# A graph-attention kernel on one core: all seven slots of a tile summed by TensorE

## The chip, the core and the metric

The kernel runs on one core of a Trainium2 chip. The metric is the device time of one execution in microseconds (us). A core has five engines with a queue of instructions each, which run side by side and meet by semaphores: TensorE (PE, with its weight loads as PEld), VectorE (DVE), ScalarE (ACT), GpSimd (POOL) and SyncE (SP). SyncE here only issues DMAs; ScalarE and POOL issue some too. Matmul results go to PSUM, everything else lies in SBUF.

## What is computed

A graph-attention layer over 8192 nodes with 256 features, a residual and a layer norm:

```python
h = features @ W
s1 = h @ a1; s2 = h @ a2
e = leaky_relu(s1[:, None] + s2[None, :], negative_slope=0.2)
e = where(adjacency > 0, e, -9e15)
attention = softmax(e, axis=1)
out = layernorm(x + elu(attention @ h))
```

The adjacency matrix is 8192 x 8192 int32, 268 MB, and sparse: the chance of an edge falls with the row and column number, so that most rows have few edges and the first ones many.

## The kernel before

Rows are taken in 64 tiles of 128 (T = 64), two tiles make a pair (G = 32 pairs). The adjacency matrix is streamed once through SBUF, in 128 halves of a tile (2 MB each), and the few edges of a row are found without ever holding the row as floats. Work runs as follows.

**First phase** (to about 150 us): TensorE projects x to h, VectorE copies it out, POOL stores it row by row into a table `haug` in DRAM, with s1 and s2 as two more columns.

**The scan**, one step s per tile. ScalarE's `count` (L1317) turns a half of the adjacency tile into bf16. TensorE's `pack` (L529) multiplies it by powers of two into `pk` in PSUM, 16 matmuls per tile. VectorE's `scan` (L771 to L805) reads the column numbers of up to eight edges per row from it and writes `ids`. POOL's `gather` (L1499) fetches the rows of h for the first K = 7 of them, one indirect DMA per slot, into `GATH`, a ring of four tiles.

**The softmax over the slots** comes some steps later (`soft_step`; in four steps two tiles come at once). VectorE's `soft_logits` (L814 to L821) makes the logits, ScalarE's L1326 the exponentials, and VectorE's `soft_weights` the seven weights. The weighted sum of the seven gathered rows is split. For four slots (ON_PE) VectorE writes four diagonal matrices `diag` (L835) and TensorE's `slots` (L540) multiplies each with its gathered rows, adding up in a bank of `acc`. For the other three VectorE itself multiplies and adds into `PART` (L842, L845 twice). `aggregate` (L851) adds the two parts for a pair. ScalarE takes the exponential of the sum (L1337), VectorE's `residual` (L859 to L874) makes the elu and adds x, POOL makes the inverse standard deviation (L1511, L1513), VectorE's `normalise` (L880) finishes and SyncE stores the pair (L453).

**Rows with more than seven edges** are done densely in 16 chunks beside the scan (`mid_` functions): the first tile, and 128 listed rows. TensorE's part of it is a spread of s2 (L582), transposes (L596) and sums (L606), VectorE's among others L924 and L952, ScalarE's L1352, L1357 and L1368. In one of three steps TensorE has the sums and the spread behind the slots.

**The order** is written out by hand, per engine and step. TensorE: two packs, the slots of the step before, the dense pieces. VectorE: `normalise`, `soft_weights`, the scan, `soft_logits`, `residual`, `aggregate`, dense pieces. SyncE has one queue: the loads of the halves, each waiting until the count of three halves before is through (four buffers), and every store placed after a fixed load. After the last step VectorE's order for the last three tiles is written out singly.

```python
dve.wait_ge(sum_ready, t - 1)                     # diag(t): the sums of two tiles before
pe.wait_ge(agg_ready, j - 1)                      # slots of pair j: the addition of pair j - 2
pool.wait_ge(sum_ready, t - RING + 1)             # gather(t): the ring
pool.wait_ge(part_steps, PARTS * (t - RING + 1))
```

Of the kernel before, what the change touches and what calls it, by code (L numbers as in the profile page):

```python
# [23 lines left out]
ON_PE = 4  # L24
# [11 lines left out]
def gat_resnorm(nc, x, adj, W, attn, out):  # L36
# [21 lines left out]
    with ExitStack() as ctx:  # L58
# [26 lines left out]
        diag = sb("diag", [P, 2, 4, P], F32)  # L85
        PART = sb("PART", [P, 2, GROUP, D], F32)
# [73 lines left out]
        probsT = [diag[:, b, :, :].rearrange("p a b -> p (a b)") for b in range(2)]  # L160
# [102 lines left out]
        part_steps = sem("part_steps")  # L263
        sum_ready = sem("sum_ready")
        agg_ready = sem("agg_ready")
# [143 lines left out]
        PARTS = K - ON_PE  # L409
# [70 lines left out]
        def _(pe):  # L480
# [53 lines left out]
            def slots(t):  # L534
                j = t // 2
                pe.wait_ge(diag_ready, t + 1)
                if j >= 2:
                    pe.wait_ge(agg_ready, j - 1)
                for k in range(ON_PE):
                    done = nc.tensor.matmul(acc[:, j % 2, (t % 2) * D:(t % 2 + 1) * D], diag[:, t % 2, k, :],  # L540
                                            GATH[:, t % RING, k * DA:k * DA + D],
                                            start=(k == 0), stop=(k == ON_PE - 1))
# [193 lines left out]
        def _(dve):  # L736
# [87 lines left out]
            def soft_weights(t):  # L824


                r, b, j = t % RING, t % 2, t // 2
# [5 lines left out]
                if t >= 2:  # L833
                    dve.wait_ge(sum_ready, t - 1)
                dve.tensor_tensor(diag[:, b, 0:ON_PE, :], ident[:].unsqueeze(1).broadcast_to([P, ON_PE, P]),  # L835
                                  weight[:, 0:ON_PE].unsqueeze(2).broadcast_to([P, ON_PE, P]), ALU.mult)\
                    .then_inc(diag_ready, 1)
                part = PART[:, j % 2, b, :]
                for k in range(ON_PE, K):
                    rows = GATH[:, r, k * DA:k * DA + D]  # L840
                    if k == ON_PE:
                        dve.tensor_scalar(part, rows, weight[:, k:k + 1], None, ALU.mult).then_inc(part_steps, 1)  # L842
                    else:
                        dve.wait_ge(part_steps, PARTS * t + k - ON_PE)
                        dve.scalar_tensor_tensor(out=part, in0=rows, scalar=weight[:, k:k + 1], in1=part,  # L845
                                                 op0=ALU.mult, op1=ALU.add).then_inc(part_steps, 1)

            def aggregate(j):
                dve.wait_ge(sum_ready, 2 * j + 2)
                dve.wait_ge(part_steps, PARTS * (2 * j + 2))  # L850
                dve.tensor_tensor(PART[:, j % 2, :, :], acc[:, j % 2, :].rearrange("p (u d) -> p u d", u=GROUP),  # L851
# [835 lines left out]
```

## Time and profile before

| | us |
|---|---|
| median of 3 runs | 853.82 |
| lowest, highest | 851.44, 854.61 |
| the profiled execution | 854.12 |
| its span, first to last instruction | 852.3 |
| busy: PE, DVE, ACT, POOL | 602.2, 612.7, 578.0, 603.0 |

The four compute engines are each busy 68 to 72% of the span. The DMA engines moved 320 MB, 376 GB/s on average. A stretch's "DMA share" is the mean busy share of the 16 DMA engines, where 1.0 means that they are full; the "granted clock" is the share of TensorE's full clock, and one instruction sees either the full one (2.4 GHz) or the half (1.2 GHz). In the rows an idle time in brackets names who ended it.

### The profile page before, as it was taken

Reading aid. Unit: us, or ns where it says so; the run is one execution under the profiler, and the core shown is the slowest. Engines: PE = TensorE matmul, PEld = TensorE weight load, DVE = VectorE, ACT = ScalarE, POOL = GpSimd, SP = SyncE. Lnnn points to the kernel's source line nnn. Section 1 sums busy time; section 2 is a strip of 40 time slices with the busy share of each in tenths; the row PEclk is TensorE's granted clock in tenths of the full one; section 3 lists DMA queues with packets and bytes.
Section 4 is the critical chain, followed back from the end, with each engine's and each line's share of the span. In section 5 each row is a group of like instructions: output and inputs, shape, how many; then the busy total and the mean of one; then the engine's idle time right before and its main releaser. Section 6 shows DMA issues by size and latency. Waiting matters only on the chain.

```text
span 852.3 us, 10622 instructions
## 1 busy us (share of the span) xinstructions
PE 602.2 (71%) x2585; PEld 384.6 (45%) x2628; DVE 612.7 (72%) x2382; ACT 578.0 (68%) x531; POOL 603.0 (71%) x689
## 2 busy tenths in 40 slices
PE   6598887466967668787786746688668685776761
PEld 5466663333645335453553424445345352443430
DVE  4247563287689767778897679678877867888784
ACT  3034546388788777887787678768877886797710
POOL 4487425778778776777774777778878786878762
PEclk9799998799889897896988979799998997988875
DMA  8999997999999999999999999999999998999611
GB/s 323 401 406 399 375 390 302 416 403 416 412 416 417 415 418 415 416 419 397 382 376 425 413 373 420 409 348 374 408 419 413 415 415 338 399 412 411 252 26 44
DMA packets 62849, 320.20 MB, mean 376 GB/s; under 512 B 19286, under 2 KB 37943, under 8 KB 46400
## 3 DMA queue, kind: packets, MB, share of 16 engines
q1 hardware_dynamic: 36176, 285.49, 82.2%
q0 software_dynamic: 25456, 29.79, 10.5%
q10 hardware_dynamic: 1152, 4.19, 1.3%
q8 instruction: 23, 0.38, 0.2%
q14 instruction: 42, 0.34, 0.1%
HBM read 344.79 MB, written 17.14 MB: 425 GB/s over the span
## 4 chain that ended last, share of the span: by engine, by line
DMA 27%; DVE 21%; issue 21%; PE 15%; POOL 12%; ACT 2%; POOLq 0%; SPq 0%; ACTq 0%; DVEq 0%
POOL GATH L1499 10%; DMA ADJ<-in_adj_dram 9%; DMA GATH<-haug,ids 8%; PE acc L515 6%; DMA WORK<-in_adj_dram,smalls 5%; PE pk L529 4%; DMA X<-in_x_dram 3%; PE acc L540 2%; DVE diag L835 2%; DMA out_dram<-Y 2%; DVE GATH L762 2%; ACT WORK L1317 2%; DVE PART L845 2%; DVE smalls L776 1%; DVE Y L863 1%
## 5 line engine op out<-in xcount | busy, mean ns | idle before, releaser
L1317 ACT ACTIVATE WORK<-ADJ 128x4096 bf16<-128x4096 int32 x128 | 462.1, 3611 | 156.1 <-PE pk L529 79.4
L1499 POOL DMA_INDIRECT GATH<-haug,ids x448 | 468.7, 1046 | 133.2 <-issue 129.2
L529 PE MATMUL pk<-WORK,D 128*128 128x512 bf16 x981 | 267.9, 423 | 146.8 <-ACT WORK L1317 143.6
L529 PEld LDWEIGHTS pk<-WORK,D 128*128 128x128 bf16 x1024 | 101.0, 105 | 288.6 <-ACT WORK L1317 171.9
L540 PE MATMUL acc<-GATH,diag 128*128 128x256 f32 x512 | 149.2, 443 | 56.0 <-DVE diag L835 56.0
L540 PEld LDWEIGHTS acc<-GATH,diag 128*128 128x128 f32 x512 | 114.9, 229 | 96.5 <-DVE diag L835 71.0
L515 PE MATMUL acc<-Waug,GATH 128*128 128x258 f32 x256 | 66.2, 403 | 11.9 <-DVE GATH L762 11.8
L771 DVE MAX8 smalls<-pk 128x8 f32<-128x512 f32 x64 | 44.5, 695 | 32.1 <-issue 32.1
L845 DVE SCALAR_TENSOR_TENSOR PART<-GATH,smalls,PART 128x256 f32<-128x256 f32 x128 | 62.2, 486 | 4.5
L515 PEld LDWEIGHTS acc<-Waug,GATH 128*128 128x128 f32 x256 | 48.9, 198 | 24.7 <-issue 16.8
L606 PE MATMUL mid_acc<-X,WORK 128*128 128x256 f32 x256 | 59.0, 384 | 0.0
L1472 POOL DMA_DIRECT2D haug<-GATH x32 | 23.5, 734 | 48.8 <-DVE GATH L762 48.7
L606 PEld LDWEIGHTS mid_acc<-X,WORK 128*128 128x128 f32 x256 | 49.5, 193 | 7.2
L814 DVE TENSOR_SCALAR smalls<-GATH,S 128x7 f32<-128x7 f32 x64 | 16.8, 262 | 46.1 <-DMA GATH<-haug,ids 46.0
L1468 POOL TENSOR_TENSOR GATH<-GATH,X 128x512 f32<-128x512 f32 x32 | 40.8, 1276 | 10.5 <-DMA X<-in_x_dram 8.6
L835 DVE TENSOR_TENSOR diag<-ident,smalls 128x512 f32<-128x512 f32 x64 | 44.4, 694 | 2.4 <-DVE smalls L831 0.2
L1326 ACT ACTIVATE smalls<-smalls 128x7 f32<-128x7 f32 x64 | 18.5, 289 | 40.0 <-DVE smalls L821 39.8
L776 DVE FIND_INDEX8 smalls<-smalls,pk 128x8 uint32<-128x512 f32 x64 | 44.3, 692 | 0.0
L1352 ACT ACTIVATE WORK<-WORK,smalls 128x1024 f32<-128x1024 int32 x16 | 18.2, 1140 | 26.8 <-DMA WORK<-in_adj_dram,smalls 26.8
L761 DVE COPY S<-acc 128x4 f32<-128x4 f32 x32 | 5.2, 162 | 42.5 <-PE acc L515 42.4
L1337 ACT ACTIVATE Y<-PART 128x512 f32<-128x512 f32 x32 | 19.8, 619 | 23.2 <-DMA out_dram<-Y 12.8
L582 PE MATMUL xT_ps<-WORK,ident 64*128 64x128 f32 x256 | 33.4, 282 | 0.0
(165 smaller groups left out, 762.2 us busy)
## 6 DMA issues: line engine op xcount, KB each, us to landing
ADJ<-in_adj_dram SPq DMA_DIRECT2D x128, 2048.0 KB
haug<-GATH POOLq DMA_DIRECT2D x32, 258.0 KB, 8.6
out_dram<-Y SPq DMA_DIRECT2D x32, 256.0 KB, 11.7
GATH<-haug,ids POOLq DMA_INDIRECT x448
X<-in_x_dram SPq DMA_DIRECT2D x1, 4096.0 KB, 32.5
WORK<-in_adj_dram ACTq DMA_DIRECT2D x8, 512.0 KB, 10.9
X<-in_x_dram SPq DMA_DIRECT2D x1, 3072.0 KB, 27.1
X<-in_x_dram SPq DMA_DIRECT2D x1, 1024.0 KB, 6.4
```

What stands on the lines that cost most here:

```text
L515: done = nc.tensor.matmul(acc[:, u, 0:DA], XT[g % 2][:, at:at + P], Waug[:, c, :], start=(c == 0), stop=(c == C - 1))
L529: done = nc.tensor.matmul(pk[s % PKS][:], D16[:, k, :], A16[:, q % 2, k * BW:(k + 1) * BW], start=(half == 0 and k == 0), stop=(half == 1 ...
L540: done = nc.tensor.matmul(acc[:, j % 2, (t % 2) * D:(t % 2 + 1) * D], diag[:, t % 2, k, :], GATH[:, t % RING, k * DA:k * DA + D], start=(k ...
L582: done = nc.tensor.matmul(xT_ps[t // 4][:, (t % 4) * P:(t % 4 + 1) * P], ident[0:T, row:row + 1].broadcast_to([T, P]), s2T, start=True, st ...
L606: done = nc.tensor.matmul(mid_acc[:], mid_probsT[u // 4][:, (u % 4) * P:(u % 4 + 1) * P], X[:, c * (MW // P) + u, :], start=(u == 0), stop ...
L771: dve.max(vals[:, 0:FOUND], pk[s % PKS][:]).then_inc(scan_steps, 1)
L776: dve.max_index(places, vals[:, 0:FOUND], pk[s % PKS][:]).then_inc(scan_steps, 1)
L835: dve.tensor_tensor(diag[:, b, 0:ON_PE, :], ident[:].unsqueeze(1).broadcast_to([P, ON_PE, P]), weight[:, 0:ON_PE].unsqueeze(2).broadcast_t ...
L845: dve.scalar_tensor_tensor(out=part, in0=rows, scalar=weight[:, k:k + 1], in1=part, op0=ALU.mult, op1=ALU.add).then_inc(part_steps, 1)
L1317: act.activation(A16[:, q % 2, :], ADJ[:, q % 4, :], ACT.Relu, scale=HALF_SCALE if q % 2 else 1.0, accum_out=degree[:, q // 2, q % 2:q % 2 ...
L1468: pool.tensor_tensor(x_sum, x_sum, X[:, GROUP * g:GROUP * (g + 1), :], ALU.add).then_inc(x_summed, 1)
L1499: pool.indirect_dma_start(out=GATH[:, r, k * DA:(k + 1) * DA], out_offset=None, in_=haug, in_offset=bass.IndirectOffsetOnAxis(ap=ids[:, t ...
```

## The change

The slots that go to TensorE are all seven. `diag` grows from four to seven matrices per tile, written by one instruction of 896 columns in place of 512, and `slots` issues seven matmuls in place of four. `PART`, the three instructions per tile that filled it and `aggregate` are gone with their semaphores `part_steps` and `agg_ready`. ScalarE's exponential and the second step of `residual` read `acc` in PSUM. ScalarE waits for `sum_ready` in place of `agg_ready`. TensorE, before it overwrites a bank of `acc`, waits for `y_steps`, the second step of `residual` of two pairs before. POOL's gather waits for `sum_ready` only.

```diff
-ON_PE = 4
...
-        diag = sb("diag", [P, 2, 4, P], F32)
-        PART = sb("PART", [P, 2, GROUP, D], F32)
+        diag = sb("diag", [P, 2, K, P], F32)
...
                 if j >= 2:
-                    pe.wait_ge(agg_ready, j - 1)
-                for k in range(ON_PE):
+                    pe.wait_ge(y_steps, 4 * (j - 2) + 2)
+                for k in range(K):
                     done = nc.tensor.matmul(acc[:, j % 2, (t % 2) * D:(t % 2 + 1) * D], diag[:, t % 2, k, :],
                                             GATH[:, t % RING, k * DA:k * DA + D],
-                                            start=(k == 0), stop=(k == ON_PE - 1))
+                                            start=(k == 0), stop=(k == K - 1))
...
-                dve.tensor_tensor(diag[:, b, 0:ON_PE, :], ident[:].unsqueeze(1).broadcast_to([P, ON_PE, P]),
-                                  weight[:, 0:ON_PE].unsqueeze(2).broadcast_to([P, ON_PE, P]), ALU.mult)\
+                dve.tensor_tensor(diag[:, b, :, :], ident[:].unsqueeze(1).broadcast_to([P, K, P]),
+                                  weight.unsqueeze(2).broadcast_to([P, K, P]), ALU.mult)\
                     .then_inc(diag_ready, 1)
-                part = PART[:, j % 2, b, :]
-                for k in range(ON_PE, K):
-                    rows = GATH[:, r, k * DA:k * DA + D]
-                    if k == ON_PE:
-                        dve.tensor_scalar(part, rows, weight[:, k:k + 1], None, ALU.mult).then_inc(part_steps, 1)
-                    else:
-                        dve.wait_ge(part_steps, PARTS * t + k - ON_PE)
-                        dve.scalar_tensor_tensor(out=part, in0=rows, scalar=weight[:, k:k + 1], in1=part,
-                                                 op0=ALU.mult, op1=ALU.add).then_inc(part_steps, 1)
-
-            def aggregate(j):
-                dve.wait_ge(sum_ready, 2 * j + 2)
-                dve.wait_ge(part_steps, PARTS * (2 * j + 2))
-                dve.tensor_tensor(PART[:, j % 2, :, :], acc[:, j % 2, :].rearrange("p (u d) -> p u d", u=GROUP),
-                                  PART[:, j % 2, :, :], ALU.add).then_inc(agg_ready, 1)
...
-                dve.scalar_tensor_tensor(out=Y[:, b, :, :], in0=PART[:, b, :, :], scalar=0.0, in1=Y[:, b, :, :],
+                dve.scalar_tensor_tensor(out=Y[:, b, :, :], in0=acc[:, b, :].rearrange("p (u d) -> p u d", u=GROUP),
+                                         scalar=0.0, in1=Y[:, b, :, :],
                                          op0=ALU.max, op1=ALU.add).then_inc(y_steps, 1)
...
-                act.wait_ge(agg_ready, j + 1)
+                act.wait_ge(sum_ready, 2 * j + 2)
...
-                act.activation(Y[:, b, :, :], PART[:, b, :, :], ACT.Exp).then_inc(elu_ready, 1)
+                act.activation(Y[:, b, :, :], acc[:, b, :].rearrange("p (u d) -> p u d", u=GROUP), ACT.Exp).then_inc(elu_ready, 1)
...
                     pool.wait_ge(sum_ready, t - RING + 1)
-                    pool.wait_ge(part_steps, PARTS * (t - RING + 1))
```

TensorE around the third of the four double steps, where the sums of two tiles (L540) stand ahead of the dense sums (L606), the spread (L582) and the next two packs (L529), before:

```order
L529 MATMUL pk<-WORK,D 128x512 x16
L540 MATMUL acc<-GATH,diag 128x256 x8
L606 MATMUL mid_acc<-X,WORK 128x256 x8
L582 MATMUL xT_ps<-WORK,ident 128x128 x8
L529 MATMUL pk<-WORK,D 128x512 x16
L540 MATMUL acc<-GATH,diag 128x256 x4
```

and after, where the lines of the same operations have other numbers:

```order
L524 MATMUL pk<-WORK,D 128x512 x16
L535 MATMUL acc<-GATH,diag 128x256 x14
L601 MATMUL mid_acc<-X,WORK 128x256 x8
L577 MATMUL xT_ps<-WORK,ident 128x128 x8
L524 MATMUL pk<-WORK,D 128x512 x16
L535 MATMUL acc<-GATH,diag 128x256 x7
```

Six matmuls more stand between one pair of packs and the next in a double step, three in any other.

VectorE from the weights of the last tile but one to the `normalise` (L880) that stands ahead of the last tile's logits, before (L829 to L845 are `soft_weights`, L851 is `aggregate`, L999 to L1008 dense rows):

```order
L829 RECIPROCAL smalls<-smalls 128x1 [waits exp_ready]
L831 TENSOR_SCALAR smalls<-smalls 128x7 [waits weight_steps]
L835 TENSOR_TENSOR diag<-ident,smalls 128x512 [waits sum_ready,weight_steps]
L842 TENSOR_SCALAR PART<-GATH,smalls 128x256
L845 SCALAR_TENSOR_TENSOR PART<-GATH,smalls,PART 128x256 [waits part_steps] x2
L851 TENSOR_TENSOR PART<-acc,PART 128x512 [waits part_steps,sum_ready]
L999 SCALAR_TENSOR_TENSOR WORK<-WORK 128x256 [waits mid_x_loaded,mid_h_copied,mid_elu]
L1002 SCALAR_TENSOR_TENSOR WORK<-WORK 128x256 [waits mid_y_steps]
L1005 BN_STATS smalls<-WORK 128x6 [waits mid_y_steps]
L1007 MEMSET smalls 128x1 [waits mid_y_steps]
L1008 BN_AGGR smalls<-smalls 128x2
L880 TENSOR_SCALAR Y<-Y,smalls 128x256 [waits rstd_ready]
```

and after:

```order
L824 RECIPROCAL smalls<-smalls 128x1 [waits exp_ready]
L826 TENSOR_SCALAR smalls<-smalls 128x7 [waits weight_steps]
L830 TENSOR_TENSOR diag<-ident,smalls 128x896 [waits sum_ready,weight_steps]
L980 SCALAR_TENSOR_TENSOR WORK<-WORK 128x256 [waits mid_x_loaded,mid_h_copied,mid_elu]
L983 SCALAR_TENSOR_TENSOR WORK<-WORK 128x256 [waits mid_y_steps]
L986 BN_STATS smalls<-WORK 128x6 [waits mid_y_steps]
L988 MEMSET smalls 128x1 [waits mid_y_steps]
L989 BN_AGGR smalls<-smalls 128x2
L861 TENSOR_SCALAR Y<-Y,smalls 128x256 [waits rstd_ready]
```

Four instructions are gone between the diagonals and the dense rows' step, and `diag` is written in one wider instruction.

## Rows read from the trace of the kernel before

**Rows 1.** Stretches: start:end, length, busy PE, PEld, DVE, ACT, POOL, PEclk, DMA share, GB/s

```profile
150.00:400.00 250.00, 175.14 (x731) 109.41 (x745) 186.79 (x761) 192.10 (x181) 189.36 (x210) 0.86 1.02 415
400.00:435.00 35.00, 26.65 (x123) 17.23 (x123) 31.29 (x121) 28.34 (x28) 28.04 (x31) 0.86 0.95 366
...
550.00:590.00 40.00, 31.91 (x136) 21.09 (x137) 33.48 (x131) 30.84 (x29) 32.55 (x39) 0.90 0.94 357
...
700.00:725.00 25.00, 14.45 (x60) 8.18 (x60) 18.78 (x78) 15.39 (x16) 16.30 (x19) 0.80 0.90 348
...
800.00:852.30 52.30, 20.42 (x69) 12.26 (x68) 35.45 (x128) 11.07 (x16) 25.99 (x34) 0.73 0.14 41
```

**Rows 2.** Page, costliest groups: line, engine, op, shapes, count | busy, mean ns | idle

```profile
L1499 POOL DMA_INDIRECT GATH<-haug,ids x448 | 468.7, 1046 | 133.2 <-issue 129.2
...
L540 PE MATMUL acc<-GATH,diag 128*128 128x256 f32 x512 | 149.2, 443 | 56.0 <-DVE diag L835 56.0
...
L845 DVE SCALAR_TENSOR_TENSOR PART<-GATH,smalls,PART 128x256 f32<-128x256 f32 x128 | 62.2, 486 | 4.5
...
L835 DVE TENSOR_TENSOR diag<-ident,smalls 128x512 f32<-128x512 f32 x64 | 44.4, 694 | 2.4 <-DVE smalls L831 0.2
...
L842 DVE TENSOR_SCALAR PART<-GATH,smalls 128x256 f32<-128x256 f32 x64 | 22.4, 351 | 0.0
...
L851 DVE TENSOR_TENSOR PART<-acc,PART 128x512 f32<-128x512 f32 x32 | 21.9, 686 | 0.0
```

**Rows 3.** Waits: engine, what waited <- for whom: us in total, times, longest

```profile
PE acc L540 <- DVE diag L835: 56.0, 26, 7.3
...
SPq L453 <- DVE Y L880: 219.4, 32, 22.1
```

**Rows 4.** Timeline at a double step: start, us, engine, line, operation, count [idle before]

```profile
548.78 3.62 ACT L1317 ACTIVATE WORK<-ADJ 128x4096 bf16<-128x4096 int32 x1
...
549.58 5.74 PE L540 MATMUL acc<-GATH,diag 128*128 128x256 f32 x14
...
557.82 0.39 SPq L453 DMA_DIRECT2D out_dram<-Y  x1
...
560.90 3.40 PE L529 MATMUL pk<-WORK,D 128*128 128x512 bf16 x15 [0.16 <-issue]
...
562.67 3.62 ACT L1317 ACTIVATE WORK<-ADJ 128x4096 bf16<-128x4096 int32 x1 [2.41 <-PE pk L529]
...
564.14 1.89 PE L540 MATMUL acc<-GATH,diag 128*128 128x256 f32 x8
```

**Rows 5.** Timeline of the last tiles, all engines

```profile
823.10 3.78 PE L540 MATMUL acc<-GATH,diag 128*128 128x256 f32 x8 [2.36 <-DVE diag L835]
...
826.01 1.00 POOL L1499 DMA_INDIRECT GATH<-haug,ids  x1 [0.30 <-issue]
...
831.04 0.22 DVE L814 TENSOR_SCALAR smalls<-GATH,S 128x7 f32<-128x7 f32 x1
...
832.78 0.69 DVE L835 TENSOR_TENSOR diag<-ident,smalls 128x512 f32<-128x512 f32 x1
...
833.53 2.76 PE L540 MATMUL acc<-GATH,diag 128*128 128x256 f32 x8 [4.07 <-DVE diag L835]
...
837.79 0.63 ACT L1337 ACTIVATE Y<-PART 128x512 f32<-128x512 f32 x1 [5.50 <-DVE PART L851]
...
838.26 0.73 DVE L880 TENSOR_SCALAR Y<-Y,smalls 128x256 f32<-128x256 f32 x2 [0.18 <-POOL smalls L1513]
...
838.91 0.68 DVE L859 SCALAR_TENSOR_TENSOR Y<-Y,X 128x512 f32<-128x512 f32 x1
```

**Rows 6.** Page, the chain that ended last: shares of the span by line

```profile
POOL GATH L1499 10%; DMA ADJ<-in_adj_dram 9%; DMA GATH<-haug,ids 8%; PE acc L515 6%; DMA WORK<-in_adj_dram,smalls 5%; PE pk L529 4%; DMA X<-in_x_dram 3%; PE acc L540 2%; DVE diag L835 2%; DMA out_dram<-Y 2%; DVE GATH L762 2%; ACT WORK L1317 2%; DVE PART L845 2%; DVE smalls L776 1%; DVE Y L863 1%
```

**Rows 7.** Timeline, the gather beside L952

```profile
758.76 1.94 POOL L1499 DMA_INDIRECT GATH<-haug,ids  x1 [0.30 <-issue]
```

**Rows 8.** DMA issues: line, queue, count, KB each, us from issue to landing

```profile
haug<-Y POOLq DMA_DIRECT2D x1, 1.0 KB, 2.2
```

More of the change, by code:

```diff
@@ L159, in gat_resnorm @@
             .rearrange("p (t q) -> p t q", t=TH)
-        probsT = [diag[:, b, :, :].rearrange("p a b -> p (a b)") for b in range(2)]
+        probsT = [diag[:, b, 0:TB, :].rearrange("p a b -> p (a b)") for b in range(2)]
         d16_flat = D16[:].rearrange("p k q -> p (k q)")
@@ L262, in gat_resnorm @@
         diag_ready = sem("diag_ready")
-        part_steps = sem("part_steps")
         sum_ready = sem("sum_ready")
-        agg_ready = sem("agg_ready")
         elu_ready = sem("elu_ready")
@@ L408, in gat_resnorm @@
         WEIGHTS = 2
-        PARTS = K - ON_PE
         def heavy_rows(eng):
@@ L824, in soft_weights @@
             def soft_weights(t):
-                r, b, j = t % RING, t % 2, t // 2
+                b = t % 2
                 dve.wait_ge(exp_ready, t + 1)
@@ L1122, in after_scan @@
                     residual(j)
-                for j in pairs_at(s - 1):
-                    aggregate(j)
                 mid_pieces(s)
@@ L1151, in _ @@
             soft_weights(T - 2)
-            aggregate(G - 2)
             mid_residual(1)
@@ L1157, in _ @@
             residual(G - 2)
-            aggregate(G - 1)
             mid_normalise(1)
@@ L1291, in dense_round @@
                 dve.bn_aggr(mean_var[:, 0, 0, :], stats[:, 0, :]).then_inc(dense_steps, 1)
-            dve.wait_ge(agg_ready, G)
             dve.memset(gate[:, 4:5], 0.0).then_inc(sum_taken, 1)
@@ L1615, in prepare @@
                     pool.wait_ge(sum_ready, T - 2)
-                    pool.wait_ge(part_steps, PARTS * (T - 2))
                 pool.indirect_dma_start(out=rows_h, out_offset=None, in_=haug, in_offset=rows,
```

## The prediction, made before the changed kernel ran

> **What bounds the kernel now.** I read the busy shares by stretch first, then the groups of the lines that change, then two places in order of time. The stretches [rows 1] give the frame. From 150 to 400 us the DMA engines are full (share 1.02, 415 GB/s) while VectorE is busy 75% (186.79 of 250) and TensorE 70%. So the adjacency stream bounds most of the scan, and an engine that gets faster there gains nothing. In three stretches the stream thins: 400 to 435 us (share 0.95, 366 GB/s), 550 to 590 (0.94, 357), 700 to 725 (0.90, 348). In the first two VectorE is busy 89% and 84%, the highest of all. After 800 us the stream is over (share 0.14) and only the chain of the last tiles counts.
>
> How can VectorE starve the stream? SyncE issues the loads of the adjacency matrix and the stores of the output in one queue. A store waits for VectorE's `normalise`, and the next load stands behind it; SyncE spent 219.4 us in such waits [rows 3]. At 557.82 us a store went out whose load behind it could have gone when ScalarE finished its second count of that step, 548.78 + 3.62 = 552.40 [rows 4]: 5.4 us late. That is VectorE's doing. TensorE is in the same place too: two tiles' slot sums (5.74 us from 549.58) and the middle-row work push the next packs to 560.90, and ScalarE's count at 562.67 waited 2.41 us for one of them [rows 4].
>
> **The change part by part.** VectorE loses, per tile, one multiply (0.351 us) and two multiply-adds (2 x 0.486), in all 1.32 us; per pair it loses the addition (0.686 us, 0.34 per tile) [rows 2]. It gains a wider `diag`: 896 columns for 512. Its price is not in the trace. By the slope between the 256 columns of L845 and the 512 of L835 (0.208 us for 256) it is 0.31 us more; in proportion to the width it is 0.694 x 384/512 = 0.52; I take 0.40, nearer to the slope since every instruction has a fixed part. Net per tile: 1.32 + 0.34 - 0.40 = 1.26 us less, 81 us of 612.7 over 64 tiles. Most of it is removed beside a full stream and is worth nothing.
>
> TensorE gains three fp32 matmuls per tile. One costs 149.2/256 = 0.58 us on average (each is two records) [rows 2]; at the full granted clock, 2.4 GHz, four take 1.89 us, 0.47 each [rows 4]; at the half, 1.2 GHz, four take 3.78, 0.95 each [rows 5]. So 1.4 to 2.8 us per tile, 1.75 on average, 112 us in all. TensorE goes from 70% to about 86% of the scan. What hides it is TensorE's wait for `diag`, 56.0 us in 26 waits [rows 3], and its waits for ScalarE's counts; but the wider `diag` lies ahead of the sums, so 0.4 us of each is not hidden by the former.
>
> The waits that change hands cost nothing by themselves. TensorE may overwrite a bank of `acc` only after the second `residual` step of two pairs before, instead of after the addition. On VectorE that step always stands ahead of the `diag` for which the same sums wait, so `diag_ready` comes last. ScalarE's exponential reads `acc` as soon as TensorE is through. POOL's gather loses the wait on the partial sums and keeps that on TensorE's, which come later: between nothing and the 1.4 to 2.8 us wherever the ring of four tiles is just full.
>
> At the double steps (four times, where two tiles' sums come in one step) both sides meet. At 550 us VectorE's path to the store loses 2 x 0.92 us (partial sums less wider `diag`) and one addition, 2.5 us; the store, and the load behind it, go 2.5 us earlier. TensorE's run of sums gets six more matmuls, 2.8 to 5.7 us, ahead of the pack on which ScalarE's count at 562.67 waits; that count, and the load after it, go later by as much. Net for the stream 0.3 to 3.2 us worse. At the single steps around 430 and 580 us it is 1.3 to 1.6 us off VectorE against 1.4 on TensorE, half hidden by the waits above. The idle share that all this can move is (1.02 - 0.95) x 35 + (1.02 - 0.94) x 40 = 5.7 us [rows 1]. I take 1.0 us gained in sum, since SyncE waits at 32 stores [rows 3] and only four steps are double; ends: 5.7 gained, 6.4 lost (two double steps at 3.2).
>
> The end is a chain that can be followed [rows 5]. The last gather is issued at 826.01 + 1.00. The logits of the last tile start at 831.04, without a wait: VectorE was late, not the gather. From the tile before, VectorE drops 2 x 0.92 + 0.69 = 2.5 us ahead of it, so the logits could start at 828.5, unless the rows land later. When they land is not shown, only that it is between 827.0 and 831.0; I take 829.2, by the small store to `haug`, which lands 2.2 us after its issue [rows 8], and gain 1.8 us (0 to 2.5). Then the last `diag` (832.78 + 0.69) ends at 833.47 - 1.8 + 0.4 = 832.1. From its end to the last `residual` (838.91) VectorE needed 5.4 us; 1.32 + 0.69 go, but TensorE's sums now stand in the path. Seven matmuls take 3.3 us at the full clock, 4.8 at the mixed rate of this place (2.76 for four) and 6.6 at the half clock; the exponential adds 0.63 and 0.1 of hand-over. VectorE itself is ready after 4.2 us (5.4 less 2.0, plus some 0.8 for which the inverse deviation from POOL then shows, since VectorE waited for it 0.18 us already at 838.26). So the last `residual` starts at 832.1 + 5.5 = 837.6 at the mixed rate, 1.3 us earlier; 836.3 at the full clock; 839.4 at the half, 0.5 later. I take 1.2 gained; ends 2.6 gained, 0.5 lost.
>
> On reading PSUM: the addition L851 has a PSUM source and takes 0.686 us, L835 of the same width has two in SBUF and takes 0.694 [rows 2], so I put nothing for the source that moves from `PART` to `acc`. The Trainium skill, "VectorE: DVE Perf Modes", section on the TRN2 errata, gives 120 cycles of fixed cost with a PSUM source and 58 without. By that the 32 instructions would cost an estimated 65 ns more each, 0.1 us of it on the end's chain; the two rows don't agree with it, and the sum by it would be 852.0 for 851.9.
>
> Sum, against the profiled execution of 854.1 us: 854.1 - 1.2 - 1.0 = 851.9. That execution has a span of 852.3 and 1.8 us around it, and stands 0.3 us above the median of the runs, 853.8, less than their spread (851.4 to 854.6).
>
> **The rivals.**
> *VectorE was the only brake.* If TensorE's additions hide in its waits, both thin stretches close: 854.1 - 1.2 - 5.7 = 847.2. For: 84 to 89% busy VectorE, a store 5.4 us late. Against: TensorE started its packs at 560.90 after a wait of only 0.16 us [rows 4], and is itself busy 80% of that stretch [rows 1].
> *TensorE becomes the brake.* In each double step under a thin stream, half-clock matmuls put the pack of the next step 5.7 us back, the store's gain gives 2.5 back, and the end's sums run at the half clock: 854.1 + 2 x 3.2 + 0.5 = 861.0. It decides once the added matmuls (six, 2.8 to 5.7 us) exceed what VectorE gives (2.5). Against: from 700 to 725 us, behind the last double step, TensorE is busy 58% only, and the mean granted clock of the two thin stretches was 0.86 and 0.90 of the full one [rows 1].
> *POOL gathers faster.* A gather instruction takes 1.046 us on average [rows 2] but 1.00 undisturbed [rows 5], and one took 1.94 [rows 7], beside VectorE's L952, which has two inputs in SBUF: 448 x 0.046 = 21 us. The gathers hold 10% of the chain [rows 6], so all of it gone is worth 2.1 us: 851.9 - 2.1 = 849.8. The Trainium skill, "SBUF — State Buffer", section "Who interferes with whom", says that a VectorE instruction with two SBUF inputs blocks a GpSimd one that reads SBUF; by that rule the trace agrees. Against: L952, behind the longest, stays, and the wider `diag` blocks for longer.
> *Nothing moves.* The stream ends when it did and the end's gain is eaten by the clock: 854.1.
>
> **How the numbers follow.** The forecast 851.9 has 0.48; VectorE alone 847.2, 0.22; TensorE the brake 861.0, 0.15; POOL 849.8, 0.06; nothing 854.1, 0.09. About 0.5% (4.3 us) is what a measurement of this kernel can tell from no change: faster means under 849.5, slower over 858.1. Faster: 0.22 + 0.08 from the better ends of the forecast and of POOL = 0.30. Slower: 0.15. Same: 0.55. The range leaves out the far half of VectorE alone and TensorE as the brake: 846.0 to 858.0.
>
> **What would show it.** VectorE busy near 532 us, TensorE near 714, the wider `diag` near 1.1 us. Right if 150 to 400 us stays at 415 GB/s and the time from the last count to the end shrinks by 1 to 2.5 us. If the thin stretches are gone, VectorE was the brake; if they grew and ScalarE's waits for `pk` did, TensorE is. The forecast is wrong if the gathers of the ring start to wait for TensorE's sums, or if the stream thins between 150 and 400 us.

## The result: 0.7% slower

The changed kernel took 857.48 us (median of 5 runs, 856.77 to 860.46) against 853.07 us for the kernel before in the same job (851.44 to 854.61). The ratio is 1.0069, 95% interval 1.0054 to 1.0085: 4.4 us at the medians and 5.9 by the ratio. The forecast was 851.9, 1.9 us under the 853.8 that it started from, with 0.15 on slower by over 0.5%. So the time moved the other way. That 857.5 still lies within the stated range of 846.0 to 858.0 is luck: its upper end was not drawn for any cause that the runs found. The profiled execution has a span of 855.7 us, 3.4 more than before.

### The profile page after: what moved, and what is told of

Same layout as the page of the kernel before. It is cut to its first block, busy times and chain, and to the rows that moved or that the text cites. A ratio compares the mean times of both kernels' runs of the same rounds, so it can differ in the third digit from the quotient of the medians.

```text
span 855.7 us, 11074 instructions
## 1 busy us (share of the span) xinstructions
PE 664.2 (78%) x2969; PEld 454.3 (53%) x3012; DVE 546.5 (64%) x2158; ACT 576.7 (67%) x531; POOL 615.6 (72%) x689
## 4 chain that ended last, share of the span: by engine, by line
issue 26%; POOL 24%; DMA 19%; PE 17%; DVE 12%; POOLq 1%; ACT 1%; SPq 0%; ACTq 0%; DVEq 0%
POOL GATH L1474 21%; DMA GATH<-haug,ids 6%; PE acc L510 6%; PE acc L535 5%; DMA ADJ<-in_adj_dram 5%; DMA WORK<-in_adj_dram,smalls 4%; DMA X<-in_x_dram 3%; PE pk L524 3%; DVE GATH L757 2%; DVE diag L830 1%; PE mid_acc L601 1%; POOL smalls L1471 1%; DVE Y L843 1%; DVE Y L839 1%; PE xT_ps L499 1%
## 5 line engine op out<-in xcount | busy, mean ns | idle before, releaser
L1474 POOL DMA_INDIRECT GATH<-haug,ids x448 | 481.2, 1074 | 131.6 <-issue 129.2
L1293 ACT ACTIVATE WORK<-ADJ 128x4096 bf16<-128x4096 int32 x128 | 461.9, 3610 | 145.4 <-PE pk L524 96.5
L524 PE MATMUL pk<-WORK,D 128*128 128x512 bf16 x981 | 245.8, 400 | 89.9 <-ACT WORK L1293 86.4
L535 PE MATMUL acc<-GATH,diag 128*128 128x256 f32 x896 | 237.1, 423 | 58.1 <-DVE diag L830 57.9
L535 PEld LDWEIGHTS acc<-GATH,diag 128*128 128x128 f32 x896 | 189.0, 214 | 110.9 <-DVE diag L830 77.0
L830 DVE TENSOR_TENSOR diag<-ident,smalls 128x896 f32<-128x896 f32 x64 | 70.0, 1094 | 2.2
L861 DVE TENSOR_SCALAR Y<-Y,smalls 128x256 f32<-128x256 f32 x64 | 24.0, 416 | 27.3 <-POOL smalls L1488 27.3
L1328 ACT ACTIVATE WORK<-WORK,smalls 128x1024 f32<-128x1024 int32 x16 | 18.2, 1137 | 34.2 <-DMA WORK<-in_adj_dram,smalls 34.2
L905 DVE CUSTOM_DVE_ANT_0 WORK<-xT_ps,WORK 128x512 f32<-128x512 f32 x32 | 20.7, 685 | 18.6 <-issue 18.6
L577 PEld LDWEIGHTS xT_ps<-WORK,ident 64*128 64x128 f32 x256 | 29.7, 187 | 5.3 <-issue 5.3
```

The lines of the kernel that those rows point to most:

```text
L524: done = nc.tensor.matmul(pk[s % PKS][:], D16[:, k, :], A16[:, q % 2, k * BW:(k + 1) * BW], start=(half == 0 and k == 0), stop=(half == 1 ...
L577: done = nc.tensor.matmul(xT_ps[t // 4][:, (t % 4) * P:(t % 4 + 1) * P], ident[0:T, row:row + 1].broadcast_to([T, P]), s2T, start=True, st ...
L830: dve.tensor_tensor(diag[:, b, :, :], ident[:].unsqueeze(1).broadcast_to([P, K, P]), weight.unsqueeze(2).broadcast_to([P, K, P]), ALU.mult)\
L861: dve.tensor_scalar(Y[:, b, u, :], Y[:, b, u, :], mean_var[:, b, u, 0:1], rstd[:, b, u:u + 1], ALU.subtract, ALU.mult).then_inc(normed, 1)
L1293: act.activation(A16[:, q % 2, :], ADJ[:, q % 4, :], ACT.Relu, scale=HALF_SCALE if q % 2 else 1.0, accum_out=degree[:, q // 2, q % 2:q % 2 ...
L1474: pool.indirect_dma_start(out=GATH[:, r, k * DA:(k + 1) * DA], out_offset=None, in_=haug, in_offset=bass.IndirectOffsetOnAxis(ap=ids[:, t ...
```

## The profile after

Stretches of after, with the columns of [rows 1] (start:end, length, busy PE, PEld, DVE, ACT, POOL, PEclk, DMA share, GB/s):

```profile
150.00:400.00 250.00, 198.27 (x863) 133.07 (x877) 166.65 (x697) 194.15 (x185) 192.50 (x209) 0.90 1.02 414
400.00:435.00 35.00, 29.52 (x150) 20.91 (x152) 26.40 (x104) 27.75 (x26) 28.22 (x31) 0.95 0.97 384
550.00:590.00 40.00, 34.81 (x155) 24.19 (x156) 27.04 (x112) 28.99 (x30) 32.23 (x38) 0.91 0.96 363
625.00:650.00 25.00, 14.50 (x64) 8.83 (x65) 12.17 (x51) 14.38 (x13) 20.28 (x23) 0.80 0.90 354
700.00:725.00 25.00, 14.44 (x56) 9.55 (x56) 12.68 (x49) 13.60 (x12) 16.17 (x19) 0.80 0.79 308
800.00:855.70 55.70, 29.29 (x113) 20.04 (x112) 33.17 (x122) 11.36 (x18) 29.74 (x39) 0.80 0.20 70
```

and the one stretch that wasn't shown of before:

```profile
625.00:650.00 25.00, 15.07 (x63) 8.06 (x62) 18.47 (x76) 20.59 (x23) 19.87 (x22) 0.86 1.02 419
```

The two thin stretches that the prediction looked at got a little better against [rows 1] (0.95 to 0.97, 0.94 to 0.96). Two others got worse: 625 to 650 us fell from 1.02 to 0.90, 700 to 725 from 0.90 to 0.79. In both VectorE and ScalarE are less busy than before and POOL about as much. Up to 550 us after is in fact ahead: its counts for tiles 31 to 38 end 2.3 to 3.1 us earlier than in before. At tile 48, at 645 us, it is 5.6 us behind, and its last count ends at 811.0 us against 810.6.

The groups of after that answer to [rows 2] (page of the profile; line, engine, op, shapes, count | busy, mean ns | idle), and one of `residual`:

```profile
L1474 POOL DMA_INDIRECT GATH<-haug,ids x448 | 481.2, 1074 | 131.6 <-issue 129.2
L535 PE MATMUL acc<-GATH,diag 128*128 128x256 f32 x896 | 237.1, 423 | 58.1 <-DVE diag L830 57.9
L830 DVE TENSOR_TENSOR diag<-ident,smalls 128x896 f32<-128x896 f32 x64 | 70.0, 1094 | 2.2
L843 DVE SCALAR_TENSOR_TENSOR Y<-acc,Y 128x512 f32<-128x512 f32 x32 | 22.1, 691 | 1.1
```

POOL's 448 gather instructions are the same, and nothing was changed on POOL but a wait; yet they take 12.5 us more in sum (468.7 before, [rows 2]). In the chain that ended last they went from 10% of the span [rows 6] to 21%, its first entry. (This share alone proves nothing: two of the faster kernels below, those with the narrow `diag`, have 18% and 17%.)

```profile
POOL GATH L1474 21%; DMA GATH<-haug,ids 6%; PE acc L510 6%; PE acc L535 5%; DMA ADJ<-in_adj_dram 5%; DMA WORK<-in_adj_dram,smalls 4%; DMA X<-in_x_dram 3%; PE pk L524 3%; DVE GATH L757 2%; DVE diag L830 1%; PE mid_acc L601 1%; POOL smalls L1471 1%; DVE Y L843 1%; DVE Y L839 1%; PE xT_ps L499 1%
```

The end, in order of time (timeline, some rows of it):

```profile
821.93 1.02 POOL L1474 DMA_INDIRECT GATH<-haug,ids  x1 [0.15 <-issue]
...
830.16 0.99 POOL L1474 DMA_INDIRECT GATH<-haug,ids  x1 [0.30 <-issue]
...
831.46 0.72 POOL L1488 TENSOR_TENSOR smalls<-smalls 128x2 f32<-128x2 f32 x1
...
832.21 0.73 DVE L861 TENSOR_SCALAR Y<-Y,smalls 128x256 f32<-128x256 f32 x2 [4.37 <-POOL smalls L1488]
...
832.86 0.22 DVE L809 TENSOR_SCALAR smalls<-GATH,S 128x7 f32<-128x7 f32 x1
...
834.60 1.09 DVE L830 TENSOR_TENSOR diag<-ident,smalls 128x896 f32<-128x896 f32 x1
...
835.75 5.47 PE L535 MATMUL acc<-GATH,diag 128*128 128x256 f32 x14 [4.53 <-DVE diag L830]
...
841.25 0.60 ACT L1313 ACTIVATE Y<-acc 128x512 f32<-128x512 f32 x1 [7.15 <-PE acc L535]
841.88 0.69 DVE L839 SCALAR_TENSOR_TENSOR Y<-Y,X 128x512 f32<-128x512 f32 x1 [1.90 <-ACT Y L1313]
```

The last tile's first gather starts 10.9 us behind the last count (821.93 - 811.0); before it was 7.5. The seventh ends at 831.15, and the inverse deviation, which stands behind it on POOL, at 832.18. VectorE, now early, waits 4.37 us for that and only then starts the last logits, at 832.86 instead of 831.04 [rows 5]. So VectorE did become free earlier, and POOL was late. The same wait grew over the whole execution (waits of after; in before it was 6.9 us, in 6 waits):

```profile
DVE Y L861 <- POOL smalls L1488: 27.3, 12, 4.5
```

## One gather, held

What POOL does differently can be read from a single place. Timeline of after at 582 us:

```profile
582.73 1.09 DVE L830 TENSOR_TENSOR diag<-ident,smalls 128x896 f32<-128x896 f32 x1
...
582.93 1.77 POOL L1474 DMA_INDIRECT GATH<-haug,ids  x1 [0.30 <-issue]
```

The gather starts 0.20 us into the `diag` and ends at 584.70, 0.88 us behind the end of the `diag` (583.82). An undisturbed one takes 1.00. It reads as if the gather needs something 0.12 us after its start and gets it only when the `diag` is through. This holds over the whole trace. Of the gathers that start from 0.05 us behind the start of a `diag` to 0.13 us ahead of its end, each single one ends 0.87 to 0.94 us behind the end of the `diag`: 43 gathers in after, of 1.54 us on average, 23 in before, of 1.33. What they take above 1.00 us is 23.0 us in after and 7.5 in before.

A wider `diag` catches more gathers, and holds each for longer. With a gather every 1.30 us, a `diag` of length d holds on average (d - 0.17) x (d - 0.17) / (2 x 1.30): 0.10 us for 0.69 and 0.33 for 1.09, or 6.7 and 20.8 us over 64 tiles (an estimate from those rows, near the 7.5 and 23.0 measured). So the 0.40 us on VectorE come with 0.24 us on POOL, per tile.

The change itself contains a comparison at equal width. The second step of `residual` reads `PART` in SBUF beside `Y` in before, and `acc` in PSUM beside `Y` in after, and is as long in both (0.693 and 0.691 us). In before 12 gathers start within it and take 1.7 us over 1.00 in sum, the longest 1.42; in after 14 do and take 0.06, the longest 1.02. One such pair from each timeline, before and then after:

```profile
601.30 0.69 DVE L863 SCALAR_TENSOR_TENSOR Y<-PART,Y 128x512 f32<-128x512 f32 x1
601.46 1.42 POOL L1499 DMA_INDIRECT GATH<-haug,ids  x1
...
410.04 0.69 DVE L843 SCALAR_TENSOR_TENSOR Y<-acc,Y 128x512 f32<-128x512 f32 x1
410.20 1.02 POOL L1474 DMA_INDIRECT GATH<-haug,ids  x1
```

## The experiments

Theory POOL: the wide `diag`, an instruction with two tensors in SBUF, holds the gathers up, POOL falls behind, and the dense rows' gathers and the last tile's come late. Rival, theory TensorE: three more matmuls per tile put the packs back. A third: the relief of VectorE itself does harm. All runs are of 5 rounds; "gathers" is the busy time of the 448 gather instructions, "held" what those that start within a `diag`, by the bounds above, take over 1.00 us each. The kernel before had a median of 852.2 to 853.1 us in the five jobs; the ratio is to the one in the same job, and times of different jobs are compared as they stand. The two right-hand columns are of the profiled execution.

| run | us | ratio to before (95%) | gathers, us | held, us | last count, us | from there to the end of the span |
|---|---|---|---|---|---|---|
| before | 853.1 | | 468.7 | 7.5 | 810.6 | 41.7 |
| after | 857.5 | 1.0069 (1.0054 to 1.0085) | 481.2 | 23.0 | 811.0 | 44.7 |
| narrow diag, four matmuls | 848.1 | 0.9952 (0.9935 to 0.9970) | 468.4 | 9.8 | 805.1 | 38.3 |
| wide diag, four matmuls | 854.0 | 1.0021 (1.0005 to 1.0037) | 482.0 | 22.0 | 806.9 | 44.5 |
| narrow diag, seven matmuls | 846.5 | 0.9929 (0.9914 to 0.9944) | 465.0 | 6.1 | 806.8 | 38.4 |
| seven singles | 851.8 | 1.0001 (0.9990 to 1.0013) | 458.9 | under 3 | 808.0 | 40.0 |
| seven pairs | 851.2 | 0.9985 (0.9974 to 0.9996) | 463.3 | under 4 | 809.3 | 40.4 |
| weights in PSUM | 846.2 | 0.9927 (0.9914 to 0.9939) | 464.3 | 4.5 | 805.0 | 39.5 |
| two parts | 848.9 | 0.9966 (0.9946 to 0.9986) | 471.0 | 11.6 | 807.0 | 40.6 |

**Which of the two additions.** The changed kernel with a narrow `diag`, with four matmuls, and with both. These three leave parts of the computation out: with four matmuls, slots five to seven are missing from the sum (and `stop` is at the fourth); the seven matmuls beside the narrow `diag` read its four matrices over again (`diag[:, t % 2, k % 4, :]`).

```diff
-                dve.tensor_tensor(diag[:, b, :, :], ident[:].unsqueeze(1).broadcast_to([P, K, P]),
-                                  weight.unsqueeze(2).broadcast_to([P, K, P]), ALU.mult)\
+                dve.tensor_tensor(diag[:, b, 0:4, :], ident[:].unsqueeze(1).broadcast_to([P, 4, P]),
+                                  weight[:, 0:4].unsqueeze(2).broadcast_to([P, 4, P]), ALU.mult)\
```

```diff
-                for k in range(K):
+                for k in range(4):
```

> The changed kernel with both of its additions taken out: diag is written for four slots (512 columns) and TensorE sums four; slots five to seven are left out of the sum. VectorE's relief stays. Both theories take the loss from one of the additions and expect a gain here: 847 to 851 us, gathers near 1.04 us on average, gathers over 1.4 us long 13 or fewer. If it is 854 or more, neither addition is the cause but the relief itself (VectorE out of step with the rest).

> The changed kernel with its wide diag (896 columns), but TensorE sums four slots; the other three are left out of the sum. Theory POOL (the wide two-input write holds POOL's gather instructions up): as slow as the changed kernel, 856 to 858 us, over 25 gathers longer than 1.4 us, the last tile's gather some 4 us behind its ids. Theory TensorE (three more matmuls per tile put the packs back): as fast as the kernel with both additions out, 847 to 852 us.

> The changed kernel with seven matmuls per tile, but diag of four slots (512 columns), of which three are used a second time; so the weights of slots five to seven are wrong in the sum. Theory POOL: 848 to 852 us, gathers near 1.045 us on average, at most 15 over 1.4 us. Theory TensorE: 856 to 859 us, TensorE busy 660 us and ScalarE's waits for pk near 95 us.

With both additions out the kernel is 0.48% faster than before: VectorE's relief is a gain, and the third theory falls. Seven matmuls beside a narrow `diag` cost nothing (846.5 against 848.1), with TensorE busy 658 us: theory TensorE falls as the main cause. The wide `diag` alone costs 6 us (854.0 against 848.1), less than theory POOL wanted (856 to 858); beside seven matmuls it costs 11 (857.5 against 846.5). The narrow one with seven, at 846.5, is under the 848 to 852 expected. The gathers follow the width, not the matmuls. The page of the kernel with the wide `diag` and four matmuls:

```profile
L1474 POOL DMA_INDIRECT GATH<-haug,ids x448 | 482.0, 1076 | 131.6 <-issue 129.5
```

and that of the kernel with the narrow one and seven:

```profile
L1474 POOL DMA_INDIRECT GATH<-haug,ids x448 | 465.0, 1038 | 132.5 <-issue 130.9
```

**Is it the hold, or VectorE's 0.40 us?** Four ways to write all seven matrices, all of them the whole computation:

```diff
+                for k in range(K):
+                    done = dve.tensor_scalar(diag[:, b, k, :], ident[:], weight[:, k:k + 1], None, ALU.mult)
...
+                for k in range(K):
+                    done = dve.tensor_tensor(diag[:, b, k, :], ident[:], weight[:, k:k + 1].broadcast_to([P, P]), ALU.mult)
...
+                wt = weight if W_SB <= t < W_SE else list_ps[:, 2 * P + 8:2 * P + 8 + K]
+                dve.tensor_scalar(wt, expd[:, b, :], rden[:, 0:1], None, ALU.mult).then_inc(weight_steps, 1)
...
+                dve.tensor_tensor(diag[:, b, 0:4, :], ident[:].unsqueeze(1).broadcast_to([P, 4, P]),
+                                  weight[:, 0:4].unsqueeze(2).broadcast_to([P, 4, P]), ALU.mult)
+                dve.tensor_tensor(diag[:, b, 4:K, :], ident[:].unsqueeze(1).broadcast_to([P, 3, P]),
+                                  weight[:, 4:K].unsqueeze(2).broadcast_to([P, 3, P]), ALU.mult)\
```

> The whole computation. The changed kernel with diag written by seven instructions of 128 columns, each the identity times one weight per partition, so that only one operand is a tensor in SBUF. Theory POOL, if the hold comes from the second tensor in SBUF: gathers beside these instructions at 1.00 us, mean 1.03 or less, time 849 to 853 us although VectorE is busy some 20 us longer. Theory TensorE: 857 us or more, since TensorE's work is the same and VectorE's grows.

> The whole computation. Diag in seven instructions of 128 columns, as in the run with seven singles, but each with two tensors in SBUF as operands (the identity and the weight, broadcast). If the second tensor in SBUF holds the gathers: gathers stretched more than beside the singles (mean over 1.05 us, over 20 of them beyond 1.2 us), time 856 us or more. If it is the length of one instruction: gathers like beside the singles, mean 1.02 to 1.03 us, none beyond 1.2 us beside a diag, time 852 to 855 us, since VectorE is longer busy still.

> The whole computation. The changed kernel with the seven weights written to free columns of a PSUM bank for 51 of the 64 tiles, so that the 896-wide diag has one tensor in SBUF and one in PSUM. If the second tensor in SBUF is the cause: one diag still 1.1 us, gathers near 1.02 us on average, under 8 of them over 1.4 us, time 844 to 849 us, below both kernels. If the width of the write or VectorE's time is the cause: 856 us or more and gathers as in the changed kernel.

> The whole computation. Diag in two instructions, 512 and 384 columns, both operands in SBUF as in the changed kernel. If a gather is held to the end of one instruction only: fewer gathers over 1.4 us (under 20), time 852 to 855 us. If the two hold as one: as the changed kernel or worse, 856 to 859 us, over 30 gathers beyond 1.4 us.

The weights in PSUM decide it. The seven weights go to unused columns of a PSUM bank (`list_ps`), and the instruction stays the same one, 896 columns wide and as long as before (1.086 us for 1.094), and the time falls from 857.5 to 846.2. Its trace has its own control, since 13 of the tiles (20 to 32) kept their weights in SBUF. The same gather in the same place as above, beside a `diag` with the weights in PSUM:

```profile
582.54 1.09 DVE L832 TENSOR_TENSOR diag<-ident,list_ps 128x896 f32<-128x896 f32 x1
...
582.78 1.00 POOL L1476 DMA_INDIRECT GATH<-haug,ids  x1 [0.30 <-issue]
```

and one beside a `diag` with both operands in SBUF, in the same execution:

```profile
428.15 1.09 DVE L832 TENSOR_TENSOR diag<-ident,smalls 128x896 f32<-128x896 f32 x1
...
428.31 1.81 POOL L1476 DMA_INDIRECT GATH<-haug,ids  x1 [0.30 <-issue]
```

1.00 us against 1.81. Of the 43 gathers that start within a `diag` of the first kind (36 by the bounds above), none took over 1.07 us; the seven that by these bounds start within one of the second took 1.60 on average and all ended 0.87 to 0.89 us behind its end. There were 15 gathers over 1.4 us in the whole execution, though, where under 8 were expected: five stand beside a `diag` of the second kind and ten beside other VectorE instructions with two tensors in SBUF, most of them the dense rows' long one. The Trainium skill, "SBUF — State Buffer", section "Who interferes with whom", says that a VectorE instruction with two inputs in SBUF blocks a GpSimd one that reads SBUF; by that rule the trace agrees. The same section reports a probe in which `tensor_tensor` did not stall a DMA, and infers as the reason that making descriptors needs the write interface, which `tensor_tensor` leaves free. Here a `tensor_tensor` held 43 of 43 gather instructions, and the measurement decides.

The width counts as the length of one instruction. In two parts (0.69 and 0.56 us) the hold falls from 23.0 to 11.6 us, where the same estimate gives 10.4, and the time to 848.9, better than the 852 to 855 expected. In seven pairs, each of two tensors in SBUF, the held time is under 4 us: a gather gets through between two of them. Here I had expected 852 to 855 from the length alone, and it was 851.2. The singles are not free of the hold: the 62 gathers that start within a tile's seven took 2.7 us over 1.00 in sum, the longest 1.12, where 1.00 each was expected. Both runs of seven are 5 us slower than the weights in PSUM with as little hold, though: VectorE needs about 1.50 us per tile for the seven (timeline of the pairs),

```profile
584.61 1.50 DVE L831 TENSOR_TENSOR diag<-ident,smalls 128x128 f32<-128x128 f32 x7
584.77 1.01 POOL L1474 DMA_INDIRECT GATH<-haug,ids  x1 [0.31 <-issue]
```

where one wide instruction needs 1.09. So VectorE's time is not free either. The intervals of singles and pairs touch (851.8 and 851.2 us). So at 128 columns the second operand costs nothing to speak of: it counts when one such instruction lasts long.

**Is POOL's time what the kernel feels?** In the kernel with the weights in PSUM, POOL's small gate addition is issued twice:

```diff
                 pool.tensor_tensor(pool_gate, minus_half[:, 0:1], minus_half[:, 0:1], ALU.add)\
                     .then_inc(pool_gated, 1)
+                pool.wait_ge(pool_gated, 2 * t + 1)
+                pool.tensor_tensor(pool_gate, minus_half[:, 0:1], minus_half[:, 0:1], ALU.add)\
+                    .then_inc(pool_gated, 1)
```

> The whole computation. The kernel with the weights in PSUM, and POOL's small gate addition (0.216 us) ahead of each tile's gathers issued twice: some 0.25 to 0.3 us more of POOL per tile, near the 0.27 by which the changed kernel's gathers were longer (481.2 - 464.3 us over 64 tiles), while VectorE and TensorE are left as they are. Theory POOL (its lost time is the whole cause): back at 854 to 858 us. If POOL's time is not what matters (the hold hurts in another way, or the gain of the weights in PSUM is VectorE's): 846 to 848 us.

It took 867.3 us, ratio 1.0169 (1.0141 to 1.0198), 21 us more than without, where 854 to 858 was expected. The dose was larger than meant: POOL's groups show 16.3 us for the second addition, and its gathers' idle time rose from 130.9 to 152.5,

```profile
L1479 POOL DMA_INDIRECT GATH<-haug,ids x448 | 463.5, 1035 | 152.7 <-issue 152.5
...
L1476 POOL TENSOR_TENSOR smalls<-smalls 128x1 f32<-128x1 f32 x64 | 16.3, 255 | 5.0
```

in all 37.9 us, or 0.59 per tile. So 0.56 us of time per us of POOL. The changed kernel's gathers take 16.9 us more than those with the weights in PSUM (481.2 - 464.3), and its time is 11.3 us more: 0.67 per us. The two agree in size, with nothing changed on VectorE or TensorE in the one and nothing on POOL in the other.

**Where it arises.** The weights in PSUM for a part of the tiles only (`33 <= t < 58`, then `t >= 58`):

> The whole computation. The changed kernel with the weights in PSUM for tiles 33 to 57 only. Of the 11 us between the changed kernel and the one with the weights in PSUM for 51 tiles, some 6 lie in the stream (last count at 811.0 against 805.0) and 5 behind it (44.8 against 39.5). If the stream's part arises in the thin places after 430 us: last count at 805 to 807, time 848 to 852 us. If it arises before 400 us: last count at 809 to 811, time 854 or more.

> The whole computation. The changed kernel with the weights in PSUM for tiles 58 to 63 only. If POOL's backlog at the end is made by the last few tiles alone: last count near 811 as in the changed kernel, from there to the end 40 us in place of 44.8, time 851 to 854 us. If the backlog is carried in from earlier tiles: 43 to 45 us behind the last count, time 855 to 858 us.

Tiles 33 to 57 give nearly all of it: 847.8 us, ratio 0.9947 (0.9928 to 0.9965), with the last count at 806.3 and the span's end 39.5 us behind it. The last six tiles alone give the end (39.7 us behind the last count for 44.7) and do nothing for the stream (last count at 813.1, for 811.0): 854.2 us, ratio 1.0018 (1.0001 to 1.0035). Taking the holds of tiles 0 to 19 and 58 to 63 away as well (846.2) gives only 1.6 us more, so the early ones, beside a full stream, cost little. (Tiles 20 to 32 keep their weights in SBUF in both.) The loss has two parts, the stream thinned behind 600 us and the last tile's gathers. POOL's backlog at the end needs both the earlier and the last tiles' holds, since either one taken away alone removes it.

How a late POOL thins the stream can be read in the two stretches that got worse. The dense rows' adjacency comes by an indirect DMA on POOL (L1532), in the same queue as the gathers. ScalarE's L1328 waits for it to land, and ScalarE's next counts, which free the buffers of the adjacency stream, stand behind L1328. Timeline of after:

```profile
640.16 1.15 ACT L1328 ACTIVATE WORK<-WORK,smalls 128x1024 f32<-128x1024 int32 x1 [8.21 <-DMA WORK<-in_adj_dram,smalls]
...
714.76 1.15 ACT L1328 ACTIVATE WORK<-WORK,smalls 128x1024 f32<-128x1024 int32 x1 [11.40 <-DMA WORK<-in_adj_dram,smalls]
```

The two waits for the same pieces were 2.3 and 8.5 us in before, 3.7 and 7.7 with the weights in PSUM, and 8.2 and 11.4 again with the wide `diag` and four matmuls. Tile 48's last count, 5.6 us behind, stands right after the first of them. The issue was 3.3 us later than in before (625.33 for 622.00), and the rest of the delay lies between issue and landing, which the runs don't explain.

**And the kernel before?** The same edit in it, for 46 tiles:

> The whole computation. The kernel before with its weights in PSUM for 46 of the 64 tiles, all else as it was: 512-wide diag, partial sums on VectorE. If the second tensor in SBUF holds the gathers there too: gathers near 1.03 us on average (from 1.046), time 1 to 4 us lower, 848 to 851. If not: 852 to 853 us.

Its gathers went from 468.7 to 465.9 us, and the time stayed: 852.6, ratio 1.0010 (0.9990 to 1.0029). The second outcome, then. Nor did the last 4.6 us of gathers bring anything in the weights-in-PSUM kernel, where the 13 tiles' `diag` and the dense rows' 1.27 us instruction (L933) were cut in two:

> The whole computation. The kernel with the weights in PSUM, its 13 tiles with weights in SBUF written by two instructions, and the dense rows' 1.27 us instruction with two tensors in SBUF (L933 of the changed kernel) cut in two halves. Theory POOL: nearly all remaining long gathers gone, mean 1.015 us or less, time 842 to 846 us. If what is left of the holds is covered: 846 to 847 us.

Gathers 459.7 us (mean 1.026, not 1.015), 847.1 us, ratio 0.9931 (0.9911 to 0.9951), as without. So POOL's time counted between the changed kernel's 481.2 us of gathers and some 465, and neither below that in the changed kernel nor at 466 to 469 in the one before. Where the limit lies was not measured further.

**The matmuls beside late gathers.** From four to seven matmuls the narrow `diag` lost nothing, the wide one 3.5 us. Three more, so ten, in both (the sums are then not the computation's):

> The changed kernel with ten matmuls per tile in place of seven (the first three slots are added twice, so the sums are not the computation's). If TensorE's added time counts where the gathers are late: another 3 to 5 us, 860 to 863 us. If TensorE's time has no part in the loss: 856 to 858 us, as the changed kernel.

> As the run before it, but with diag of four slots (512 columns), used over again, so the weights in the sum are wrong. If TensorE's time counts only beside late gathers: 846 to 848 us, as with seven matmuls. If TensorE has no room left in either: 850 us or more, and then the comparison says nothing on the gathers.

862.0 us, ratio 1.0105 (1.0078 to 1.0133), and 851.9, ratio 0.9984 (0.9967 to 1.0001): 4.5 and 5.4 us more than with seven. Beyond seven TensorE has no room left in either, so this pair can't tell the two readings apart. Why the step from four to seven costs 3.5 us beside the wide `diag` alone stays open; it is a third of the loss at most, and in after POOL's gathers wait for TensorE's sums once, for 0.3 us, so it isn't the ring. The wide `diag` costs 10 to 11 us at seven and at ten matmuls, and 6 at four.

## The prediction, step by step

**Right:** the price of the wide `diag`, 0.40 us (1.094 - 0.694); no price for reading PSUM (`residual`'s second step 0.691 us from `acc`, 0.693 from `PART`); the full stream up to 400 us (414 GB/s); that TensorE's waits can hide its added matmuls. The Trainium skill, "VectorE: DVE Perf Modes", section on the TRN2 errata, which the prediction cites, gives 120 cycles of fixed cost with a PSUM source and 58 without; the 0.691 and 0.693 us don't show it, and the measurement decides. VectorE's relief was worth more than its terms: 848.1 and 846.5 against 852.2 us are 4 and 6 us, where the prediction summed to 2.2. Without the hold (weights in PSUM) the kernel took 846.2, near the 847.2 of the rival "VectorE was the only brake", but not by its mechanism. Of the two thin stretches that it wanted closed, 400 to 435 us went from a DMA share of 0.95 to 0.98 and 550 to 590 stayed (0.94, then 0.93); most of the gain came later: the counts were 2.8 us ahead of before at tile 46 and 5.6 at the last, with 700 to 725 going from 0.90 to 0.96.

**Wrong: the term of the wide `diag`.** This is the step that failed: it was counted as 0.4 us on VectorE, and its price on POOL was put at nothing. The rival "POOL gathers faster" had the mechanism in hand, with the 1.94 us gather of [rows 7] beside L952, and drew the wrong sign from it. It counted what is taken away (the partial sums, whose L845 also has two tensors in SBUF) and left the wider `diag` as half a sentence. In the trace of before, the gathers that start within one of the L845 (0.49 us each) took 1.3 us over 1.00 in all, within L842 0.4, within L851 0.1, and within the second step of `residual` 1.7. Those 3.4 us went away, and the `diag` added 15.5: the short ones don't make up for the long one. The hold rose from 7.5 to 23.0 us, and the gathers' time by 12.5 in after, by 16.2 against the narrow `diag` with seven matmuls. At the 0.56 us per us of the gate run the latter is 9 us of the 11 that separate 857.5 from 846.5. In the prediction's own terms: it took 1.0 us off for the stream and 1.2 for the end. Without the hold these were 5.6 (last count at 805.0 for 810.6) and 2.2 (39.5 us behind it for 41.7); the hold puts 6.0 and 5.2 back (811.0 and 44.7).

**Wrong: which engine is late next.** The prediction asked what VectorE's and TensorE's paths do at the double steps and at the end, and took POOL's gathers as given in time. POOL is as busy as the others (603 of 852 us), waits for the other engines some 17 us in all between 150 and 800 us of after, and serves three consumers in one queue: the slots, the dense rows and the inverse deviation. The end's step "the rows land by 829.2" failed first: the last gather ended at 831.15, 4.1 us later than before, and `normalise` and the logits stood behind POOL, not VectorE. From the last `diag`'s end to the last `residual` it took 6.2 us (835.69 to 841.88), 0.7 more than the forecast 5.5, since the seven matmuls took 5.47 us for 4.8.

**Right in kind, wrong in size:** TensorE's matmuls. They cost (237.1 - 149.2) / 192 = 0.46 us each, near the 0.47 of the full clock [rows 4], and not 0.58; TensorE is busy 664 us, not 714. VectorE is busy 546.5, not 532: its groups fall by 80.9 us, as summed, but instructions back to back overlap in the records, so busy time falls less. The time from the last count to the end was to shrink by 1 to 2.5 us. It grew by 3.

The rival of TensorE as the brake gave 861.0 for the slower side, near the measured time, but for a reason that the runs exclude as the main one. The sign named for it, ScalarE's waits for `pk` growing with the thin stretches, would have misled: they grew from 79.4 to 96.5 us, but with the weights in PSUM they are 95.6, and that kernel is 11 us faster.

## To carry over

When an instruction gets wider, ask who it keeps out while it runs, and not only how long it takes: a VectorE instruction with two tensors in SBUF holds a GpSimd gather to its end, and by the estimate above the price grows faster than its length (7.5 us for 64 of 0.69 us, 23.0 for 64 of 1.09). Move the small operand to PSUM (846.2 us, 0.73% under the kernel before, with the change as it is) or cut the instruction in two (848.9). Before widening, look at the longest instance of the neighbour's instruction in the trace, and at what stands beside it.

## What the runs showed of the hardware

- The hold has sharp edges. Beside a `diag` with both operands in SBUF, a gather that starts up to 0.04 us behind its start is not held (it takes 1.00, and the `diag` up to 0.07 us longer); one that starts 0.05 us or more behind it is held to the end, some 1.9 us in all beside the wide one.
- The hold goes both ways. In 12 of 64 tiles of after the `diag` starts just as a gather ends (within 0.01 us), and the instruction ahead of it (L826) shows 0.37 to 0.48 us, for 0.23 elsewhere, as if VectorE waited for POOL. The next gather, 0.30 us later, is then caught in all but one of them, for 0.67 us. Timeline of after:

```profile
592.71 1.06 POOL L1474 DMA_INDIRECT GATH<-haug,ids  x1 [0.16 <-issue]
593.26 0.47 DVE L826 TENSOR_SCALAR smalls<-smalls 128x7 f32<-128x7 f32 x1
593.77 1.09 DVE L830 TENSOR_TENSOR diag<-ident,smalls 128x896 f32<-128x896 f32 x1
594.07 1.67 POOL L1474 DMA_INDIRECT GATH<-haug,ids  x1 [0.30 <-issue]
```

- Seven 128-column instructions back to back take about 1.50 us in all, though each shows 0.286 to 0.302 us, and hardly hold a gather (under 4 us in sum, in the form with two tensors in SBUF and in the form with one).
- The identity times a weight per partition in one-tensor form took 302 ns for 128 columns, the two-tensor form 286 ns: seven of either take 1.50 us, so there is no gain on VectorE from the fewer operands.
- Beside the narrow `diag`, three fp32 matmuls more per tile cost nothing in time where they took TensorE from 71 to 78% busy, and 5.4 us where they took it from 78 to 84%.
